# Adding the routed rows into two arrays by the parity of the tile, joined on VectorE at the end

## The chip, the cores and the metric

One core of a Trainium2 chip. The metric is the device time of one execution in microseconds (us), a median over runs. Engines are called PE (TensorE), DVE (VectorE), ACT (ScalarE), POOL (GpSimd) and SP (SyncE, which here only issues DMAs).

## What is computed

A decoder layer on 32 sequences of 128 rows of 256 float32: causal attention with 16 heads, a cross attention with rotations and a decay mask, and a mixture of experts, each followed by a residual addition and a layer norm. The change touches only how the last part's outputs are summed:

```python
x = _layernorm(x + attn(x, qkv_weights))
x = _layernorm(x + xattn(x, ctx, ctx, Wq, Wk, Wv))
# ffn(x): 8 experts, the best 2 of each row, plus one shared expert
probs = softmax(x @ gate_w + gate_b)
topk_probs, topk_idx = top_k(probs, 2)
hr    = einsum('bsd,edf->ebsf', x, rw1) + rb1          # 256 -> 512
out_e = einsum('ebsf,efd->ebsd', swiglu(hr), rw2) + rb2
routed_out = einsum('ebsd,bse->bsd', out_e, cw)        # cw: top-2 probabilities
x = _layernorm(x + shared_out + routed_out)
```

## The kernel before

The program is written engine by engine, with semaphores by hand. Each engine runs its instructions in the order written; a waiting instruction holds all behind it on its engine. There are three stages.

**Attention, both kinds (to about 450 us).** `step(n)` runs over the 32 sequences, about 11 us each, software-pipelined: GpSimd's step holds the rsqrt of two layer norms (L620, L624), `turn_into` (L590, the rotated keys) and L605, which adds the shared expert's bias to a row block. Each row's packet (256 values, its own row number, its experts and weights) is scattered by L611 to `sent`, sorted by expert.

**Routed tiles (about 470 to 793 us).** `sent` is worked off in TILES = 71 tiles of 128 packets, each of one expert. Tile i goes through all engines:

- ACT: `load` (L1184) fetches `xg` three tiles ahead, `out_x` (L1194) copies the transposed rows, `silu` (L1189), `out_h` (L1199), `weighted` (L1205) writes `yw`, the result times the row's gate.
- PE: `turn_x` (L987), `turn_h` (L994), `result` (L1010), `hidden` (L1001).
- DVE: `biased` (L1536), `weight_parts` (L1541), `out_y` (L1552), `rows_of` (L1547), which turns the packet's row number into `result_row`.
- POOL: `product` (L638), `tile_weight` (L642), `add_rows` (L654): an indirect DMA that adds the 128 rows of `yw` to `total` in memory, at the rows that `result_row` names.

A hardware loop (Fori) runs four tiles per round, with the tiles of the start and the end written out. In the turn of tile i the engines stand at different tiles: ACT applies silu to tile i, weights tile i-2 and loads i+3; DVE biases tile i and finishes tile i-2; POOL multiplies tile i and then issues the adding transfer of tile i-3. A row sits in two tiles (its two experts), and two adding transfers to the same row must not overlap. So `wait_rows(i)` holds transfer i until transfer i-1 has landed (`row_added`, 16 a transfer). `yw` has two buffers, so `weighted(i)` waits for transfer i-2; `result_row` has four, so `rows_of(i)` waits for transfer i-4.

```python
def wait_rows(i):                      # L648
    eng.wait_ge(yw_set, i + 1)
    eng.wait_ge(packet_row, i + 1)
    after(eng, row_added, 16 * i)
for n in range(4):                     # in the loop over k
    product(4 * k + n, n % 2)
    wait_rows(4 * k + n - 3)
    tile_weight(4 * k + n, n)
    add_rows((n + 1) % 4)
```

**The end (from 793 us).** SP waits for the last `row_added`, loads `total` in 8 quarters of four sequences (`fin`, L565, 512 KB each), and DVE and ACT normalise them (`moments`, `shifts`, POOL's `root` L685, `finish` L1238). For quarters 4 to 7 PE still computes the shared expert (`shared_hidden` L784, `shared_output` L804), with `shared_silu` on ACT (L1093), `shared_gate` (L1389) and `add_shared` (L1400) on DVE. SP stores each quarter (L570).

## Time and profile before

| | |
|---|---|
| median of 3 runs | 839.64 us (836.67 to 840.29) |
| profiled execution | 842.12 us |
| its span in the trace | 839.9 us |
| mean granted TensorE clock | 0.971 |
| PE busy | 725.7 us (86%) |
| DVE, ACT, POOL busy | 470.1, 450.1, 372.9 us (56, 54, 44%) |
| chain that ended last, DMA | 18%, of which the adding transfers 14% |

A line of the timeline gives start, duration, engine, source line, operation, output <- inputs, count, and in brackets the idle time of the engine before it with what ended it. DMA instructions on a queue (SPq, ACTq) are the issue, not the transfer. The granted clock is a fraction of 2.4 GHz: 1.00 is 2.4, 0.50 is 1.2.

### The profile page before, as it was taken

The numbers are of one execution on the slowest core, as the hardware profiler recorded it, in microseconds if no ns is written. First come the engines' busy times: TensorE is split into PE (matmuls) and PEld (weight loads), VectorE is DVE, ScalarE is ACT, GpSimd is POOL, SyncE is SP. The second block draws the span as 40 slices with busy tenths as digits, with TensorE's granted clock in tenths as the row PEclk, the third lists the DMA queues.
The fourth block names the chain that finished last, engine by engine and source line by source line (L and its number), as shares of the span: only waits on it lengthen the run. The fifth ranks groups of instructions, "written<-read, shape, count | busy, mean of one in ns | idle before, by whom it ended". The sixth has DMA issues, their size and how long they took to land.

```text
span 839.9 us, 19432 instructions
## 1 busy us (share of the span) xinstructions
PE 725.7 (86%) x5464; PEld 527.5 (63%) x5465; DVE 470.1 (56%) x1427; ACT 450.1 (54%) x1242; POOL 372.9 (44%) x523
## 2 busy tenths in 40 slices
PE   7969999999999999999799887877887777777893
PEld 6757888888888888888555454444444443443452
DVE  3554778988888888887555333332233333332164
ACT  0367888888888888886231143333333333332135
POOL 1001333355454455554447055555555555555211
PEclk9988999999999999999899899999999999999996
DMA  8635542123222333335435633333433334333363
GB/s 298 243 113 152 199 137 64 58 90 90 73 81 84 94 100 95 103 103 175 138 110 189 198 56 64 59 65 59 63 63 63 63 63 63 60 62 43 78 223 125
DMA packets 79479, 89.43 MB, mean 106 GB/s; under 512 B 12016, under 2 KB 72048, under 8 KB 78384
## 3 DMA queue, kind: packets, MB, share of 16 engines
q1 hardware_dynamic: 55504, 59.83, 22.8%
q0 software_dynamic: 13680, 19.20, 13.1%
q10 hardware_dynamic: 10224, 9.49, 4.2%
q8 instruction: 39, 0.64, 0.3%
q14 instruction: 32, 0.26, 0.1%
HBM read 51.71 MB, written 36.77 MB: 105 GB/s over the span
## 4 chain that ended last, share of the span: by engine, by line
PE 50%; DMA 18%; issue 13%; DVE 6%; POOL 6%; ACT 3%; ACTq 2%; SPq 1%; POOLq 0%; DVEq 0%
DMA total<-oT,result_row 14%; PE ps L764 5%; POOL total L654 5%; PE ps L1001 4%; PE ps L861 4%; PE ps L752 4%; PE ps L774 4%; PE ps L729 4%; PE ps L885 3%; PE ps L864 3%; PE ps L732 3%; PE ps L804 2%; PE ps L695 2%; PE ps L784 2%; PE ps L871 2%
## 5 line engine op out<-in xcount | busy, mean ns | idle before, releaser
L1001 PE MATMUL ps<-first_use,xgT 128*128 x284 | 142.9, 626 | 53.3 <-ACT xgT L1194 53.3
L1076 ACT ACTIVATE prob<-ps,nmax 128x128 f32<-128x128 f32 x512 | 146.9, 379 | 31.2 <-DVE nmax L1275 31.2
L654 POOL DMA_INDIRECT total<-oT,result_row x71 | 112.1, 1579 | 21.9 <-issue 9.7
L1001 PEld LDWEIGHTS ps<-first_use,xgT 128*128 128x128 f32 x284 | 49.0, 191 | 114.6 <-issue 114.5
L1205 ACT ACTIVATE oT<-yg,weight 128x256 f32<-128x256 f32 x71 | 36.1, 508 | 127.3 <-DMA total<-oT,result_row 126.6
L1275 DVE TENSOR_REDUCE nmax<-ps 128x4 f32<-128x512 f32 x128 | 82.2, 685 | 25.8 <-PE ps L752 24.8
L590 POOL TENSOR_TENSOR rot<-products 128x128 f32<-128x128 f32 x128 | 61.1, 498 | 65.3 <-DVE products L1285 65.2
L1536 DVE TENSOR_TENSOR tile_parts<-ps,attn_only 128x512 f32<-128x512 f32 x71 | 49.1, 692 | 72.5 <-issue 59.7
L1083 ACT COPY pT<-ps 128x512 f32<-128x512 f32 x128 | 76.9, 601 | 19.5 <-PE ps L764 13.6
L764 PE MATMUL ps<-tf,prob 128*128 128x128 f32 x512 | 78.8, 277 | 6.1 <-ACT pT L1083 6.1
L1547 DVE CAST result_row<-xg 128x1 uint32<-128x1 f32 x71 | 10.9, 153 | 125.6 <-DMA total<-oT,result_row 125.6
L611 POOL DMA_INDIRECT sent<-packets,pos x64 | 63.4, 990 | 36.9 <-PE ps L752 22.6
L1010 PE MATMUL ps<-first_use,ghT 128*128 x284 | 73.8, 382 | 3.1 <-ACT ghT L1199 3.1
L638 POOL TENSOR_TENSOR tile_parts<-tile_parts 128x256 f32<-128x256 f32 x71 | 52.1, 733 | 47.3 <-ACT tile_parts L1189 47.3
L764 PEld LDWEIGHTS ps<-tf,prob 128*128 128x128 f32 x512 | 59.4, 142 | 12.7 <-issue 5.0
L1194 ACT COPY xgT<-ps 128x256 f32<-128x256 f32 x71 | 26.4, 372 | 70.7 <-issue 50.7
L784 PE MATMUL ps<-prob,sw_sb 128*128 128x512 f32 x128 | 58.8, 607 | 1.8 <-DVE tile_parts L1389 1.8
L1010 PEld LDWEIGHTS ps<-first_use,ghT 128*128 128x128 f32 x284 | 48.3, 190 | 7.7 <-issue 3.9
L642 POOL TENSOR_TENSOR weight<-weight_part,xg 128x1 f32<-128x1 f32 x71 | 13.4, 189 | 84.9 <-DMA total<-oT,result_row 79.8
L987 PEld LDWEIGHTS ps<-tf,xg 128*128 128x128 f32 x142 | 16.7, 143 | 53.9 <-issue 43.3
L1285 DVE TENSOR_TENSOR products<-ps,tf 128x256 f32<-128x256 f32 x128 | 46.3, 404 | 6.9 <-PE ps L864 2.4
L624 POOL TENSOR_TENSOR rstd<-mv,neg_half 128x1 f32<-128x1 f32 x32 | 17.6, 550 | 67.3 <-DVE mv L1293 67.3
(137 smaller groups left out, 1456.6 us busy)
## 6 DMA issues: line engine op xcount, KB each, us to landing
xg<-sent ACTq DMA_DIRECT2D x68, 130.5 KB, 2.1
k_dram<-first_use SPq DMA_DIRECT2D x4, 1024.0 KB, 5.7
attn_only<-in_x_turned SPq DMA_DIRECT2D x32, 128.0 KB, 3.1
attn_only<-k_dram SPq DMA_DIRECT2D x256, 16.0 KB
attn_only<-in_x SPq DMA_DIRECT2D x32, 128.0 KB, 2.7
attn_only<-in_ctx SPq DMA_DIRECT2D x32, 128.0 KB, 2.7
first_use<-in_L_ffn_rw SPq DMA_DIRECT2D x8, 512.0 KB, 5.0
x2T_dram<-x2T SPq DMA_DIRECT2D x32, 128.0 KB, 2.6
```

Source lines behind the costliest of these rows:

```text
L590: eng.tensor_tensor(rot[:, t % 2, m + e, :], ra[:, t % 2, m + e, :], rb[:, t % 2, m + 1 - e, :], ALU.add).then_inc(done, 1)
L611: eng.indirect_dma_start(sent, bass.IndirectOffsetOnAxis(ap=pos[:, t, j:j + 1], axis=0), packets[:, t % SLOTS, :], None).then_inc(sent_in[ ...
L638: eng.tensor_tensor(gate_h[:, r, :], hid[:, r, FFN:2 * FFN], sil[:, r, :], ALU.mult).then_inc(gh_set, 1)
L654: eng.indirect_dma_start(total, bass.IndirectOffsetOnAxis(ap=result_row[:, slot:slot + 1], axis=0), yw[:, slot % 2, :], None, compute_op=A ...
L764: mm = eng.transpose(PROBT[:, n * P:(n + 1) * P], prob[:, t % 2, 4 * u + n, :], ident)
L784: mm = eng.matmul(ps[:, bank + half, :].rearrange("p (b t) -> p b t", b=QB), sw1_sb[:, c, cols:cols + P], x2T4[:, q % EARLY, :, c, :], sta ...
L1001: mm = eng.matmul(ps[:, r, :], xgT[:, r, c, :], rw1_sb[:, bass.ds(e * (DC * 2 * FFN) + c * 2 * FFN, 2 * FFN)], start=(c == 0), stop=(c == ...
L1010: mm = eng.matmul(ps[:, 4 + r, 0:D], ghT[:, r, c, :], rw2_sb[:, bass.ds(e * (FFN // P * D) + c * D, D)], start=(c == 0), stop=(c == FFN // ...
L1076: ins = eng.activation(prob[:, t % 2, 4 * u + n, :], SCORE[u][:, n * P:(n + 1) * P], ACT.Exp, bias=nmax[:, t % 2, 4 * u + n:4 * u + n + 1])
L1083: eng.copy(pT[:, u, :, :].rearrange("p n t -> p (n t)"), PROBT).then_inc(pT_set, 1)
L1275: eng.tensor_reduce(nmax[:, t % 2, 4 * u:4 * u + 4], SCORE[u].rearrange("p (h j) -> p h j", j=P), AX_X, ALU.max, negate=True).then_inc(max ...
L1536: eng.tensor_tensor(hid[:, r, :], ps[:, r, :], rb_h[:, bass.ds(e * (2 * FFN), 2 * FFN)], ALU.add).then_inc(hid_set, 1)
```

## The change

`total` becomes two arrays, `totals[0]` and `totals[1]`. The transfer of an even tile adds to the first, that of an odd tile to the second, and each waits for the transfer two tiles ahead, which is the last one into the same array. The semaphore `row_added` becomes two. `totals[0]` holds what `total` held; `totals[1]` starts as zeros, written by one more transfer on POOL at step 8. At the end SP loads both, and DVE adds the second to the first (`join`) before the moments or the shared addition of that quarter. The second half of a quarter goes to parts of `first_use` and `attn_only` that the experts' weights and biases held.

```diff
-            def wait_rows(i):
+            def wait_rows(i, r, added):
                 eng.wait_ge(yw_set, i + 1)
                 eng.wait_ge(packet_row, i + 1)
-                after(eng, row_added, 16 * i)
+                after(eng, row_added[r], 16 * added)
...
-                eng.indirect_dma_start(total, bass.IndirectOffsetOnAxis(ap=result_row[:, slot:slot + 1], axis=0),
-                                       yw[:, slot % 2, :], None, compute_op=ALU.add).then_inc(row_added, 16)
+                eng.indirect_dma_start(totals[slot % 2], bass.IndirectOffsetOnAxis(ap=result_row[:, slot:slot + 1], axis=0),
+                                       yw[:, slot % 2, :], None, compute_op=ALU.add).then_inc(row_added[slot % 2], 16)
...
-                    wait_rows(4 * k + n - 3)
+                    wait_rows(4 * k + n - 3, (n + 1) % 2, 2 * k + (n - 3) // 2)
...
+                if n == 8:
+                    eng.dma_start(totals[1][:, :].rearrange("(n p) d -> p n d", p=P),
+                                  zeros[:, 0:D].unsqueeze(1).broadcast_to([P, B + 1, D])).then_inc(idle_sent, 16)
...
-            def weighted(i, r, slot):
+            def weighted(i, r, slot, added):
-                after(eng, row_added, 16 * (i - 1))
+                after(eng, row_added[r], 16 * added)
...
-                        weighted(i - 2, n % 2, (n - 2) % 4)
+                        weighted(i - 2, n % 2, (n - 2) % 4, 2 * k + (n - 2) // 2)
...
-            def rows_of(i, slot):
-                after(eng, row_added, 16 * (i - 3))
+            def rows_of(i, slot, added):
+                after(eng, row_added[slot % 2], 16 * added)
...
-            eng.wait_ge(row_added, 16 * TILES)
+            for r in range(2):
+                eng.wait_ge(row_added[r], 16 * ((TILES + 1 - r) // 2))
             for q in range(NQ):
-                eng.dma_start(fin[:, q * QB:(q + 1) * QB, :],
-                              total[q * QB * S:(q + 1) * QB * S, :].rearrange("(b p) d -> p b d", p=P)).then_inc(fin_in[q], 16)
+                for half, place in enumerate((fin[:, q * QB:(q + 1) * QB, :], odd_of(q))):
+                    eng.dma_start(place, totals[half][q * QB * S:(q + 1) * QB * S, :].rearrange("(b p) d -> p b d", p=P)
+                                  ).then_inc(fin_in[q], 16)
...
+            def join(q):
+                eng.wait_ge(fin_in[q], 32)
+                rows = fin[:, q * QB:(q + 1) * QB, :]
+                eng.tensor_tensor(rows, rows, odd_of(q), ALU.add).then_inc(joined, 1)
...
             shared_gate(5, 0, 6)
+            join(0)
             moments(0)
+            join(1)
             shared_gate(5, 1, 0)
             moments(1)
             shifts(0)
+            join(2)
+            join(3)
+            join(4)
+            shared_gate(6, 0, 6)
             add_shared(4, 2)
-            shared_gate(6, 0, 6)
             moments(2)
             shifts(1)
+            join(5)
             shared_gate(6, 1, 0)
             add_shared(5, 4)
             moments(3)
             shifts(2)
             shared_gate(7, 0, 6)
+            join(6)
             moments(4)
             shifts(3)
             add_shared(6, 2)
+            join(7)
             shared_gate(7, 1, 0)
```

The program on POOL in the loop, two tiles of it, before (lines of before; a weight's row carries the waits of `wait_rows`):

```order
L638 TENSOR_TENSOR tile_parts<-tile_parts 128x256 [waits gh_turned,sil_set]
L411 REGISTER_ALU [waits packet_row,yw_set]
L642 TENSOR_TENSOR weight<-weight_part,xg 128x1 [waits part_set,row_added]
L654 DMA total<-oT,result_row 4224x256
L636 REGISTER_ALU
L638 TENSOR_TENSOR tile_parts<-tile_parts 128x256 [waits gh_turned,sil_set]
```

and in the changed kernel (its own line numbers):

```order
L650 TENSOR_TENSOR tile_parts<-tile_parts 128x256 [waits gh_turned,sil_set]
L418 ISA [waits packet_row,yw_set]
L654 TENSOR_TENSOR weight<-weight_part,xg 128x1 [waits part_set,row_added_even]
L666 DMA total0<-oT,result_row 4224x256
L648 REGISTER_ALU
L650 TENSOR_TENSOR tile_parts<-tile_parts 128x256 [waits gh_turned,sil_set]
L654 TENSOR_TENSOR weight<-weight_part,xg 128x1 [waits row_added_odd,part_set,packet_row,yw_set]
L666 DMA total1<-oT,result_row 4224x256
```

No instruction moved there; the semaphore waited for alternates, and with it the array.

The program on DVE at the end, from the shift of quarter 0 to the moments of quarter 2, before:

```order
L1596 SCALAR_TENSOR_TENSOR shift3<-mv3,rstd3 128x4 [waits rstd3_set]
L1400 TENSOR_TENSOR first_use<-ps,first_use 128x512 [waits sy_made,fin_in4]
L1400 TENSOR_TENSOR first_use<-ps,first_use 128x512 [waits sy_made]
L1389 SCALAR_TENSOR_TENSOR tile_parts<-ps,sb1_sb,pT 128x512 [waits sy_made,ssil_set]
L1587 BN_STATS bn3<-first_use 128x6 [waits fin_in2]
```

and in the changed kernel:

```order
L1613 SCALAR_TENSOR_TENSOR shift3<-mv3,rstd3 128x4 [waits rstd3_set]
L1596 TENSOR_TENSOR first_use<-first_use 128x1024 [waits fin_in2]
L1596 TENSOR_TENSOR first_use<-first_use 128x1024 [waits fin_in3]
L1596 TENSOR_TENSOR first_use<-first_use,attn_only 128x1024 [waits fin_in4]
L1401 SCALAR_TENSOR_TENSOR tile_parts<-ps,sb1_sb,pT 128x512 [waits sy_made,ssil_set]
L1412 TENSOR_TENSOR first_use<-ps,first_use 128x512 [waits sy_made,joined]
L1412 TENSOR_TENSOR first_use<-ps,first_use 128x512 [waits sy_made]
L1604 BN_STATS bn3<-first_use 128x6 [waits joined]
```

Three joins (L1596) now stand ahead of the shared gate of (6,0) (L1401), and that gate stands ahead of the shared addition of quarter 4 (L1412).

## Rows read from the trace of the kernel before

**Rows 1.** Busy time by stretch: us, then each engine's busy us and instructions, clock, DMA, GB/s

```profile
50.00:450.00 400.00, 381.58 (x4190) 329.57 (x4191) 312.34 (x989) 304.18 (x880) 175.40 (x282) 0.97 0.35 109
...
600.00:700.00 100.00, 78.29 (x279) 41.49 (x280) 32.29 (x95) 36.86 (x95) 58.78 (x71) 1.00 0.39 62
```

**Rows 2.** Groups by line: engine, out<-in | busy us, mean ns | idle before, releaser

```profile
L1205 ACT ACTIVATE oT<-yg,weight 128x256 f32<-128x256 f32 x71 | 36.1, 508 | 127.3 <-DMA total<-oT,result_row 126.6
...
L1547 DVE CAST result_row<-xg 128x1 uint32<-128x1 f32 x71 | 10.9, 153 | 125.6 <-DMA total<-oT,result_row 125.6
```

**Rows 3.** The adding transfer's own line: durations in ns, first and last start, landing

```profile
L654 POOL DMA_INDIRECT total<-oT,result_row x71: 1550/1579/1631, 489.1 to 789.7; - x71
...
DMA to landing us min/median/max: 3.5/3.8/4.0
```

**Rows 4.** Timeline, 624 to 644: start, us, engine line op [idle before <-releaser]

```profile
624.55 1.58 POOL L654 DMA_INDIRECT total<-oT,result_row  x1 [0.15 <-issue]
...
628.48 0.51 ACT L1205 ACTIVATE oT<-yg,weight 128x256 f32<-128x256 f32 x1 [1.53 <-DMA total<-oT,result_row]
...
629.48 0.69 DVE L1536 TENSOR_TENSOR tile_parts<-ps,attn_only 128x512 f32<-128x512 f32 x1 [0.84 <-issue]
...
630.71 0.72 POOL L638 TENSOR_TENSOR tile_parts<-tile_parts 128x256 f32<-128x256 f32 x1 [0.27 <-ACT tile_parts L1189]
...
641.13 0.51 ACT L1205 ACTIVATE oT<-yg,weight 128x256 f32<-128x256 f32 x1 [1.78 <-DMA total<-oT,result_row]
...
643.82 0.71 POOL L638 TENSOR_TENSOR tile_parts<-tile_parts 128x256 f32<-128x256 f32 x1 [0.72 <-ACT tile_parts L1189]
```

**Rows 5.** Timeline, 484 to 491, before the first transfer is waited for

```profile
484.62 1.88 PE L1001 MATMUL ps<-first_use,xgT 128*128 x4
...
487.64 1.88 PE L1001 MATMUL ps<-first_use,xgT 128*128 x4
...
488.04 0.73 POOL L638 TENSOR_TENSOR tile_parts<-tile_parts 128x256 f32<-128x256 f32 x1 [2.32 <-ACT tile_parts L1189]
...
489.06 1.63 POOL L654 DMA_INDIRECT total<-oT,result_row  x1
```

**Rows 6.** Timeline, the last tiles: transfer 65

```profile
766.73 1.58 POOL L654 DMA_INDIRECT total<-oT,result_row  x1 [0.45 <-issue]
```

**Rows 7.** Timeline of the end; last, VectorE's shared gate as in Rows 2

```profile
793.28 7.43 SPq L565 DMA_DIRECT2D first_use<-total  x8
...
797.12 1.41 DVE L1587 BATCH_NORM_STATS2 bn<-first_use 128x6 f32<-128x256 f32 x4 [5.49 <-DMA first_use<-total]
...
803.61 1.29 DVE L1400 TENSOR_TENSOR first_use<-ps,first_use 128x512 f32<-128x512 f32 x2 [1.81 <-DMA first_use<-total]
...
819.70 2.07 ACT L1238 ACTIVATE first_use<-first_use,shift,rstd 128x256 f32<-128x256 f32 x4 [2.81 <-DVE shift L1596]
...
823.28 6.46 PE L804 MATMUL ps<-sw_sb,tile_parts 128*128 128x256 f32 x16 [4.99 <-DVE tile_parts L1389]
...
L1389 DVE SCALAR_TENSOR_TENSOR tile_parts<-ps,sb_sb,pT 128x512 f32<-128x512 f32 x16 | 11.9, 748 | 23.8 <-ACT pT L1093 23.8
```

**Rows 8.** DMA issues: out<-in queue op xcount, median us from issue to landing

```profile
sent<-packets,pos POOLq DMA_INDIRECT x64, 3.1
...
sent<-zeros,tail_rows POOLq DMA_INDIRECT x2, 5.1
```

**Rows 9.** Additions with both inputs in SBUF: by line, min/median/max ns

```profile
L1515 DVE TENSOR_TENSOR passed<-counts,tf x1: 752/752/752, 459.0 to 459.0; 128x568 f32<-128x568 f32 x1
...
L1448 DVE TENSOR_TENSOR res<-att,attn_only x32: 418/701/705, 59.4 to 409.5; 128x256 f32<-128x256 f32 x32
```

**Rows 10.** Transfers of zeros by line, and GpSimd's timeline at step 8

```profile
L596 POOL DMA_DIRECT2D sent<-zeros x1 | 1.2, 1191 | 27.1 <-DVE zeros L1270 27.1
...
L598 POOL DMA_DIRECT2D total<-zeros x1 | 0.6, 622 | 0.0
...
129.27 0.88 POOL L590 TENSOR_TENSOR rot<-products 128x128 f32<-128x128 f32 x2 [3.42 <-DVE products L1285]
```

More of the change, by code:

```diff
@@ L104, in decoder_kernel @@
         k_dram = nc.dram_tensor("k_dram", (B, DH, GB, 2 * DH * NU), F32).ap()
-        total = nc.dram_tensor("total", (ROWS + P, D), F32).ap()
+        totals = [nc.dram_tensor(f"total{r}", (ROWS + P, D), F32).ap() for r in range(2)]
         x2T_dram = nc.dram_tensor("x2T_dram", (B, P, DC, P), F32).ap()
@@ L271, in decoder_kernel, with odd_of @@
         fin = first_use[:, 0:B * D].rearrange("p (b d) -> p b d", d=D)
+        def odd_of(q):
+            lo = q % 4 * QB * D
+            return (first_use[:, B * D + lo:B * D + lo + QB * D] if q < 4 else attn_only[:, lo:lo + QB * D]
+                    ).rearrange("p (b d) -> p b d", d=D)
         bn3 = sb("bn3", [P, NQ, QB, 6])
@@ L369, in decoder_kernel @@
         xg_in = [sem(f"xg_in{i}") for i in range(4)]
-        row_added = sem("row_added")
+        row_added = [sem("row_added_even"), sem("row_added_odd")]
+        joined = sem("joined")
         xg_turned = sem("xg_turned")
@@ L551, in _ @@
             eng.wait_ge(zeros_laid, 16 * (NE - TAILS_SP))
-            eng.wait_ge(idle_sent, 32)
+            eng.wait_ge(idle_sent, 48)
             for i in range(3):
@@ L597, in step @@
                                   zeros[:, :].unsqueeze(1).broadcast_to([P, IDLE, PACKET])).then_inc(idle_sent, 16)
-                    eng.dma_start(total[ROWS:ROWS + P, :], zeros[:, 0:D]).then_inc(idle_sent, 16)
+                    eng.dma_start(totals[0][ROWS:ROWS + P, :], zeros[:, 0:D]).then_inc(idle_sent, 16)
+                if n == 8:
+                    eng.dma_start(totals[1][:, :].rearrange("(n p) d -> p n d", p=P),
+                                  zeros[:, 0:D].unsqueeze(1).broadcast_to([P, B + 1, D])).then_inc(idle_sent, 16)
                 t = n - 5
@@ L661, in _ @@
                 eng.wait_ge(x2_stored[r], 16 * (B - EARLY * QB) // 2)
-            eng.wait_ge(idle_sent, 32)
+            eng.wait_ge(idle_sent, 48)
             eng.wait_ge(kept_stored, 16 * EARLY)
             product(3, 1)
-            wait_rows(0)
+            wait_rows(0, 0, 0)
             tile_weight(3, 3)
@@ L675, in _ @@
                 product(i, i % 2)
-                wait_rows(i - 3)
+                wait_rows(i - 3, (i - 3) % 2, (i - 3) // 2)
                 tile_weight(i, i % 4)
@@ L679, in _ @@
             for i in range(TILES - 3, TILES):
-                wait_rows(i)
+                wait_rows(i, i % 2, i // 2)
                 add_rows(i % 4)
@@ L1231, in _ @@
             for i in range(TILES - 2, TILES):
-                weighted(i, i % 2, i % 4)
+                weighted(i, i % 2, i % 4, i // 2)
             def finish(q):
@@ L1395, in add_shared @@
                 else:
-                    eng.wait_ge(fin_in[q], 16)
+                    eng.wait_ge(joined, q + 1)
                 for i in range(2):
```

8 lines of the change are left out of this document (4 added, 4 removed).

## The prediction

> **What bounds the kernel now.** I read the busy table by stretch first [rows 1]. In the stage of the routed tiles (from about 475 us to 793) TensorE is busy 78 us of 100 at a granted clock of 1.00, GpSimd 59, the other two a third each. Before 450 TensorE is busy 95% (381.58 of 400) and the change touches only one instruction there. The groups by line [rows 2] name who waits in the tile stage: ScalarE's weighting L1205 waits 126.6 us, VectorE's row numbers L1547 125.6 us, both for the adding transfer. The row of L654 itself [rows 3] says why: 71 transfers, the first issued at 489.1, the last at 789.7, each landing 3.8 us after its issue. That is 300.67 / 70 = 4.295 us from one to the next, and it is one latency plus a short hand-over: a transfer issued at 624.55 lets L1205 start at 628.48 (3.93 us) [rows 4], and the other 0.36 are GpSimd's weight L642 and its hand-over. So the single chain transfer, landing, transfer paces the stage, and the 3.8 us are latency, of which only 1.58 occupy GpSimd [rows 3].
>
> **What the change does to that chain.** GpSimd's wait before transfer i was for the landing of i-1; now it is for i-2, the last one into the same array. The other two waits (yw on ScalarE, result_row on VectorE) asked for i-2 and i-4 already and still do, now on the semaphore of the parity. So landing, transfer is cut, and the question is what is late next. I follow what a landing still releases, in the order of the engines' programs:
> 1. Transfer i-4 lands, ScalarE weights tile i-2 (L1205), 0.51 us.
> 2. ScalarE then issues the load of tile i+3, copies xgT and applies silu to tile i+1. VectorE's bias L1536 (629.48, ends 630.17), which sits behind the waiting L1547 on VectorE, is ready at the same moment, so both engines give the same answer.
> 3. GpSimd multiplies the gates of tile i+1 (630.71, 0.72 us) and only behind this, in program order, issues the transfer of tile i-2. From the start of L1205 at 628.48 to the end of that product at 631.43 are 2.95 us [rows 4]. Product to transfer, with the weight between and no wait, is 488.04 to 489.06, thus 0.30 beyond the product's own 0.72 [rows 5].
> 4. Transfer i-2 takes 3.93 us until L1205 of tile i can start.
>
> The cycle is 2.95 + 0.30 + 3.93 = 7.18 us, and it spans two tiles: 3.59 us each. At the seam of the hardware loop the way from L1205 (641.13) to the product's end (643.82 + 0.71) is 3.40 us, 0.45 more; it falls on one parity, once in four tiles, and the in-order engines make the other parity follow: 0.11 more per tile. **The new pace is 3.70 us**, against 4.295. Two adding transfers are then in flight for part of the time, but GpSimd writes the descriptors of the second (1.58 us) while the first moves its data.
>
> Bounds of that pace. Below: TensorE alone ran tiles every 3.02 us when no transfer was yet to be waited for (L1001 at 484.62 and 487.64) [rows 5]. GpSimd alone needs 0.72 + 0.30 + 1.58 and about 0.1, 2.7 us. Both lie below 3.70. Above: an adding transfer with a second one in flight is not in the trace. The nearest rows are two plain scatters issued back to back, 3.1 us median for the 64 of L611, and 5.1 for the two of L631 [rows 8]. I take 3.93 as it stands, because the steady spacing leaves the data phases of two transfers (3.8 - 1.58 = 2.2 us each) nearly apart; every 0.1 us of latency would cost 0.05 us a tile, 3.3 us in all.
>
> **Sum for the tile stage.** Transfers 0 to 65 (489.06 to 766.73, 277.7 us) become 65 x 3.70 = 240.5: **-37**. Transfers 66 to 70 stand outside the loop: from 766.73 to the landing (SyncE's loads at 793.28) they take 26.5 us, as each waits for the one before, about 4.6 us [rows 6, 7]. With two chains I lay them out from the transfer of tile 65: tile 66 at +2.8, tile 67 at +7.1 (behind the product of tile 70, as above), tile 68 at +8.5 (it has no product ahead of it), 69 at +11.6 (67's landing is late), 70 at +13.2, landing at +17; with the 0.3 us that these unrolled waits cost in each of the five rows, +18: **-8.5**. TensorE is in time for that: even with the shared-expert matmuls that stand between its last tiles I put the result of tile 70 at about +10, before +12 where its weighting can start.
>
> **What it adds at the end.** SyncE now loads both arrays, 16 transfers of 512 KB instead of 8, in pairs. Counted from SyncE's first issue at 793.28: the first was used at 797.12 (3.8 us), the fifth at 803.61 (10.3 us), 1.62 us each [rows 7]. Pair q is then there at 2.2 + 3.24 (q + 1): 5.4, 8.7, 11.9, 15.2, 18.4, 21.6 and so on, as against 10.3 for quarter 4 alone. Each join is an addition of 128x1024 from two SBUF inputs; the nearest row is L1515, 128x568, 752 ns [rows 9], so about 1.23 us, eight of them.
> VectorE's program, same clock: the join of quarter 4 waits until 18.4 and sits ahead of the gate of (6,0), which nothing in its data requires. Join 19.6, gate 20.4, shared addition of quarter 4 done 21.7; the moments of quarter 2 start there. From there in program order, with moments and shift 2.25 (four statistics are 1.41 of it), gate 0.75, shared addition 1.3 [rows 7]: moments 24.0, join of 5 25.2 (26.2, see below), gate (6,1) 27.0, addition 28.3, moments 30.5, gate (7,0) 31.3, join of 6 32.8, moments 35.1. ScalarE's finish of quarter 3 (2.07) and silu (7,1) (some 0.7) follow those and let gate (7,1) end at 38.6, while the addition of 6 and the join of 7 fit beside them. The last 16 matmuls L804 take 6.46 us, after 4.99 us without matmuls; that gap would be about 4 again, I take the same 6.5, and they end at 45.2, where before they ended at 36.5 (829.74), and what follows is unchanged. **Tail: +8.5.** If the loads' wait alone is hidden it is +5; if TensorE's other late groups run that slowly too, +12.
>
> In that list the join of quarter 5 starts with GpSimd's root of quarter 2 (about 1 us). In the trace the addition L1448, with both inputs in SBUF, takes 418 ns at the least and 701 at the median, where GpSimd's L590 runs beside it [rows 9]. Hence the extra microsecond there and 0.3 at quarter 6. The Trainium skill, "SBUF — State Buffer", on the shared ports, says that a VectorE instruction with two SBUF inputs and a GpSimd instruction that reads SBUF exclude each other; the trace agrees (418 against 701 ns). For the loads another page speaks against my term: "DMA: Bandwidth & Descriptors" gives 436 GB/s behind a fixed 2 us, 1.20 us for a load of 512 KB. By that the pair of quarter 4 would be there about 4 us earlier and the tail would be an estimated +5; the row says 1.62 us and it decides.
>
> **What it adds at the start.** One transfer of zeros, 4224 rows, on GpSimd at step 8. Two of its kind are in the trace: 896 rows 1.19 us to issue, 128 rows 0.62 [rows 10], so 0.74 ns a row and 3.7 us for this one. At that place, ahead of L605, it delays only what stands before the 3.42 us that GpSimd idles ahead of L590 [rows 10], which hides all but 0.3. Its 4.3 MB travel in the background and are awaited only at 470 us. I charge 0.5 us, 0 to 5 if GpSimd has to wait for room for its descriptors, since then the roots of the next layer norm are late.
>
> **Rivals.**
> - *TensorE sets the pace*: if steps 2 and 3 shrink, the floor is 3.02 plus the seam, 3.15 us. Then 65 x 0.55 = 36 us less: 767. Against it stands that the rows show the way from L1205 to the product at 2.95 us with no slack to lose.
> - *Transfers in flight lengthen each other a little*: latency 4.2 to 4.5 instead of 3.93, as the additions read and write memory and the tile loads run beside them: pace 3.84 to 3.99, and with 1 or 2 us in the last five 813 to 824.
> - *Slower*: they lengthen each other as the two of L631 did, 5.1 us to landing. Pace (2 x (5.2 + 3.25) + 0.45) / 4 = 4.34: +4 us up to tile 65, the last five -5, tail and start +9, in all 848. It decides from a landing of about 4.9 us on: there the pace is 4.24, and 8 us gained (2 and 6) meet the 9 paid. L611's 3.1 us with two in flight speaks against it.
> - *The change doesn't take the order away*: another wait (yw_set, which waits for the landing two back, or the queue itself) still lines up each transfer behind the last one; pace 4.29, only the tail and start are paid, 849. The cycle above is this wait, with two tiles in it; it would need one in it.
>
> **How the numbers follow.** -37 - 8.5 + 8.5 + 0.5 = -36.5 on the profiled execution's 842.12 (span 839.9 and 2.2 around it), 805.6. The profiled one lies 2.5 above the median of 839.64, so against the median: **803.1 us**. Chances: this case 0.75, TensorE's pace 0.07, somewhat longer transfers 0.12, much longer 0.03, order kept 0.03. Within the first case the pace may be off by 0.12 (8 us), the tail by 4 us and the start by 4: 791 to 815. The range takes in most of the longer transfers: 788 to 820. Faster by over 0.5%, about what a measurement of this kernel can tell from no change, 0.93; within 0.5% 0.01; slower 0.06.
>
> **What the profile would show.** Transfers L666 spaced unevenly in pairs, 3.7 us in the mean, landing still 3.8 us; GpSimd's weight waiting for ScalarE's silu or yw rather than the transfer; ScalarE's wait at the weighting still there but below 100 us; SyncE's loads issued near 748 us, and 55 us from there to the end; VectorE waiting about 2 us for the pair of quarter 4. A landing above 4.5 us or a spacing near 4.3 would prove me wrong; a spacing near 3.1 would mean the cycle is shorter than I read it.

## The result and the profile after

The kernel after takes 802.25 us (median of 4 runs, 801.57 to 807.89), the kernel before beside it 839.96 us (4 runs, 836.67 to 842.14): a ratio of 0.957, 95% interval [0.952, 0.962]. That is faster, by about the amount forecast (803.1). The profiled execution took 801.57 us with a span of 799.7.

First the busy table by stretch, then the adding transfer's own line (durations in ns, first and last start, who waited for it in us and times, time to landing).

```profile
600.00:700.00 100.00, 87.55 (x329) 50.01 (x328) 37.04 (x108) 41.74 (x108) 67.10 (x84) 1.00 0.45 73
```

```profile
L666 POOL DMA_INDIRECT total<-oT,result_row x71: 1550/1580/1631, 486.4 to 739.5; - x71
...
who waited for it (us, times):
  ACT oT L1217: 78.9, 64
...
DMA to landing us min/median/max: 3.6/3.8/4.4
```

TensorE is busy 87.55 us of 100 at the same granted clock of 1.00, against 78.29 in [rows 1]. The 71 transfers now span 253.1 us instead of 300.7, that is 3.615 us from one to the next, and each still lands after 3.8 us [rows 3]. The transfer costs what it cost; it is waited for less. ScalarE's weighting waited 126.6 us for it in [rows 2] and 78.9 now. It still waits, so the landing has not left the path.

GpSimd's timeline of four tiles, and ScalarE's weightings of the same stretch (start, us, engine line, idle before and its releaser):

```profile
600.76 1.57 POOL L666 DMA_INDIRECT total<-oT,result_row  x1 [0.16 <-issue]
602.76 0.72 POOL L650 TENSOR_TENSOR tile_parts<-tile_parts 128x256 f32<-128x256 f32 x1 [0.42 <-ACT tile_parts L1201]
603.45 0.18 POOL L654 TENSOR_TENSOR weight<-weight_part,xg 128x1 f32<-128x1 f32 x1
603.79 1.58 POOL L666 DMA_INDIRECT total<-oT,result_row  x1 [0.16 <-issue]
607.22 0.71 POOL L650 TENSOR_TENSOR tile_parts<-tile_parts 128x256 f32<-128x256 f32 x1 [1.85 <-ACT tile_parts L1201]
...
608.25 1.57 POOL L666 DMA_INDIRECT total<-oT,result_row  x1 [0.16 <-issue]
```

```profile
604.62 0.51 ACT L1217 ACTIVATE oT<-yg,weight 128x256 f32<-128x256 f32 x1 [1.68 <-DMA total<-oT,result_row]
...
607.62 0.51 ACT L1217 ACTIVATE oT<-yg,weight 128x256 f32<-128x256 f32 x1 [0.31 <-DMA total<-oT,result_row]
```

This is the cycle of the forecast. The transfer of 600.76 lets the weighting start at 604.62 (3.86 us); silu and then the product (607.22) follow it, and the product ends at 607.93, 3.31 us after the weighting began; the transfer two tiles on starts at 608.25, 0.32 later. That is 7.49 us for two tiles. The other parity goes 603.79, 607.62, 611.10: 7.31. The weight L654 no longer waits before a transfer; the product waits for ScalarE's silu, which stands behind the weighting that waits for the landing.

The end, as SyncE's loads, VectorE and TensorE show it:

```profile
743.14 10.14 SPq L574 DMA_DIRECT2D first_use<-total  x9
```

```profile
762.28 1.22 DVE L1596 TENSOR_TENSOR first_use<-first_use,attn_only 128x1024 f32<-128x1024 f32 x1 [1.78 <-DMA attn_only<-total]
763.43 0.74 DVE L1401 SCALAR_TENSOR_TENSOR tile_parts<-ps,sb_sb,pT 128x512 f32<-128x512 f32 x1
...
776.73 0.75 DVE L1401 SCALAR_TENSOR_TENSOR tile_parts<-ps,sb_sb,pT 128x512 f32<-128x512 f32 x1 [2.71 <-ACT pT L1105]
...
783.32 0.75 DVE L1401 SCALAR_TENSOR_TENSOR tile_parts<-ps,sb_sb,pT 128x512 f32<-128x512 f32 x1 [0.39 <-ACT pT L1105]
```

```profile
784.21 5.36 PE L816 MATMUL ps<-sw_sb,tile_parts 128*128 128x256 f32 x16 [4.65 <-DVE tile_parts L1401]
```

Counted from 743.14, the join of quarter 4 starts at 19.1 after a wait for its second load, the last gate at 40.2, the last matmuls end at 46.4 and the span at 56.6. Before, the same way from SyncE's first load (793.28, [rows 7]) to the end of the span took 46.6.

The balance between the two profiled executions:

| stretch | before | after | difference | forecast |
|---|---|---|---|---|
| start of transfer 0 | 489.06 | 486.42 | -2.6 | +0.5 |
| transfers 0 to 65 | 277.7 | 239.7 | -38.0 | -37 |
| transfer 65 to SyncE's loads | 26.5 | 17.1 | -9.5 | -8.5 |
| loads to end of span | 46.6 | 56.6 | +10.0 | +8.5 |
| around the span | 2.2 | 1.9 | -0.3 | 0 |

One profile of this study, that of the kernel with one semaphore below, is of an execution slower than the timed ones (862.06 us against a median of 851.59), mostly before the tiles; its spacing and tail are read, its time is not.

The first row is no effect of the change that I could tell: the programs of this study are nearly alike up to there (one transfer of zeros more or less, and the order of the first products), and transfer 0 starts between 483.5 and 497 us, up to 4.3 us apart for kernels that ran on one chip, and 12 with that slower profile. So the experiments below are compared by the spacing of the transfers (first to last start, by 70) and the tail (SyncE's first load to the end of the span), and by their ratio to the kernel before on their own chip.

### The profile page after: what moved, and what is told of

Same layout as the page of the kernel before. It is cut to its first block, busy times and chain, and to the rows that moved or that the text cites. A ratio compares the mean times of both kernels' runs of the same rounds, so it can differ in the third digit from the quotient of the medians.

```text
span 799.7 us, 19370 instructions
## 1 busy us (share of the span) xinstructions
PE 710.9 (89%) x5464; PEld 527.2 (66%) x5465; DVE 480.7 (60%) x1435; ACT 449.2 (56%) x1242; POOL 374.1 (47%) x524
## 4 chain that ended last, share of the span: by engine, by line
PE 45%; issue 14%; DMA 13%; POOL 9%; DVE 8%; SPq 4%; ACT 3%; DVEq 1%; ACTq 1%; POOLq 1%
DMA total<-oT,result_row 9%; POOL total L666 7%; PE ps L776 5%; PE ps L764 4%; PE ps L873 4%; PE ps L786 4%; PE ps L741 4%; PE ps L876 3%; PE ps L744 3%; PE ps L897 3%; PE ps L816 2%; PE ps L796 2%; PE ps L883 2%; PE ps L935 2%; DVE products L1297 2%
## 5 line engine op out<-in xcount | busy, mean ns | idle before, releaser
L1013 PE MATMUL ps<-first_use,xgT 128*128 x284 | 137.3, 606 | 26.9 <-ACT xgT L1206 26.7
L666 POOL DMA_INDIRECT total<-oT,result_row x71 | 112.1, 1579 | 14.3 <-issue 12.5
L1013 PEld LDWEIGHTS ps<-first_use,xgT 128*128 128x128 f32 x284 | 50.7, 189 | 77.3 <-issue 75.7
L650 POOL TENSOR_TENSOR tile_parts<-tile_parts 128x256 f32<-128x256 f32 x71 | 51.1, 720 | 93.9 <-ACT tile_parts L1201 93.9
L1217 ACT ACTIVATE oT<-yg,weight 128x256 f32<-128x256 f32 x71 | 36.1, 508 | 81.7 <-DMA total<-oT,result_row 78.9
L999 PEld LDWEIGHTS ps<-tf,xg 128*128 128x128 f32 x142 | 17.1, 140 | 51.9 <-DMA xg<-sent 25.4
L1564 DVE TENSOR_TENSOR yg<-ps,attn_only 128x256 f32<-128x256 f32 x71 | 30.0, 423 | 29.0 <-PE ps L1022 22.3
```

What stands on the lines that cost most here:

```text
L650: eng.tensor_tensor(gate_h[:, r, :], hid[:, r, FFN:2 * FFN], sil[:, r, :], ALU.mult).then_inc(gh_set, 1)
L666: eng.indirect_dma_start(totals[slot % 2], bass.IndirectOffsetOnAxis(ap=result_row[:, slot:slot + 1], axis=0), yw[:, slot % 2, :], None, c ...
L1013: mm = eng.matmul(ps[:, r, :], xgT[:, r, c, :], rw1_sb[:, bass.ds(e * (DC * 2 * FFN) + c * 2 * FFN, 2 * FFN)], start=(c == 0), stop=(c == ...
```

## Experiments

Three groups ran, each beside the kernel before on its chip (medians 848.0, 845.8 and 840.5 us). Spacing and tail are from the profiles.

| kernel | us | ratio to before | spacing | tail |
|---|---|---|---|---|
| before | 839.96 | 1 | 4.295 | 46.6 |
| after | 802.25 | 0.957 | 3.615 | 56.6 |
| after again | 810.41 | 0.959 | 3.604 | 56.4 |
| order back by added waits | 873.65 | 1.030 | 4.53 | 54.8 |
| order back by one semaphore | 851.59 | 1.012 | 4.35 | 56.2 |
| transfer ahead of the product | 798.58 | 0.942 | 3.42 | 56.0 |
| the same with one array | 876.36 | 1.031 | 4.73 | 45.5 |
| transfer two tiles behind | 776.76 | 0.916 | 3.157 | 56.3 |
| the same with one array | 853.93 | 1.014 | 4.52 | 48.0 |
| no second loads, no joins | 805.21 | 0.953 | 3.62 | 51.3 |
| no second loads, joins kept | 805.22 | 0.951 | 3.64 | 52.5 |
| joins in another order | 806.56 | 0.950 | 3.62 | 51.1 |
| before with after's gate order | 842.69 | 1.003 | 4.33 | 47.0 |
| two tiles behind and joins reordered | 765.39 | 0.914 | 3.156 | 51.2 |

### Is it the wait, or the second array?

The theory is that the gain comes from the wait for the landing one back alone. The first test puts that wait back beside the new one.

```
                 after(eng, row_added[r], 16 * added)
+                after(eng, row_added[1 - r], 16 * (added + r))
```

> Two arrays, loads and joins as in the changed kernel, but each adding transfer again waits for the one just before it too (tile i-1). My theory, that the gain is the wait and nothing else: the spacing of the transfers goes back to 4.29 us and only the price of the end (10 us by the trace of the changed kernel) is left, 848 to 851 us. The rival, that two arrays make the transfers themselves cheaper: well under 840, towards 802.

Measured: 873.65 us, ratio 1.030 [1.022, 1.038]; the gain is gone, but where a ratio of 1.01 was foreseen, 2% more is lost. The landing is unchanged (3.8 us). GpSimd's timeline shows a part of the rest:

```profile
605.58 0.19 POOL L654 TENSOR_TENSOR weight<-weight_part,xg 128x1 f32<-128x1 f32 x1 [1.32 <-DMA total<-oT,result_row]
606.01 1.58 POOL L667 DMA_INDIRECT total<-oT,result_row  x1 [0.23 <-issue]
...
610.20 0.19 POOL L654 TENSOR_TENSOR weight<-weight_part,xg 128x1 f32<-128x1 f32 x1 [1.73 <-DVE result_row L1560]
610.84 1.58 POOL L667 DMA_INDIRECT total<-oT,result_row  x1 [0.45 <-issue]
```

Between weight and transfer GpSimd idles 0.45 us in two turns of four, where it was 0.15 [rows 4]; that time lies on the chain from landing to landing. Over the 71 tiles it is 23.0 us, 12.5 in the kernel after. The trace doesn't say which instruction takes it: the same 0.45 us stand ahead of transfer 65 of the kernel before [rows 6], where no wait was added. But this edit changes two things, the order and the number of waits, so I made it again with one semaphore for both arrays and no wait more than before (the waits on ScalarE and VectorE count on it too).

```
-        row_added = [sem("row_added_even"), sem("row_added_odd")]
+        row_added = sem("row_added")
...
-                after(eng, row_added[r], 16 * added)
+                after(eng, row_added, 16 * i)
```

> Two arrays, two loads, joins and second zeros as in the kernel after, but one semaphore for both arrays, so transfer i waits for the landing of i-1 with no wait more than the kernel before had. Theory (the wait makes the gain, and what the first reversal cost above 850 came from its added waits): spacing of the adding transfers 4.29 us as before, landing 3.8, tail of 55 to 56 us from SyncE's loads to the end, ratio 1.008 to 1.015. Rival (two arrays in themselves slow a transfer, as the first reversal could also be read): spacing about 4.5, ratio about 1.03. Rival (two arrays in themselves bring part of the gain): spacing below 4.2, ratio below 1.00.

Measured: 851.59 us, ratio 1.012 [1.009, 1.015]. Its transfers:

```profile
L665 POOL DMA_INDIRECT total<-oT,result_row x71: 1550/1580/1632, 495.7 to 800.3; - x71
...
DMA to landing us min/median/max: 3.7/3.9/4.4
```

The theory stands: with two arrays, both loads and the joins, but the old wait, the spacing is 4.35 (4.30 and 4.33 in two profiles with one array; the granted clock is 1.00 from 500 to 700 us) and the time is that of the kernel before plus the tail. The further loss of the first test went with its added wait, whatever its mechanism. Two arrays by themselves leave the landing at 3.9 us, where it was 3.8.

### What paces the stage afterwards?

The forecast says the product in front of the transfer, behind silu and the weighting, closes the cycle. So GpSimd issues the transfer ahead of the product.

```
                 for n in range(4):
-                    product(4 * k + n, n % 2)
                     wait_rows(4 * k + n - 3, (n + 1) % 2, 2 * k + (n - 3) // 2)
                     tile_weight(4 * k + n, n)
                     add_rows((n + 1) % 4)
+                    product(4 * k + n, n % 2)
```

> The changed kernel, with GpSimd's weight and adding transfer of a tile put ahead of the product of gates instead of behind it. My theory, that the pace of 3.69 us is a cycle of two tiles through landing, weighting, VectorE's bias, silu, product, transfer: silu and product (1.05 us) leave the cycle, it becomes 2.2 + 3.93 + the seam, 3.2 to 3.3 us a tile, near TensorE's own 3.15: spacing 3.2 to 3.3, time 772 to 780. The rival, that two transfers in flight are limited by the queue or the memory: spacing stays at 3.6 to 3.7 and the time at 800 to 803.

Measured: 798.58 us, ratio 0.942 [0.933, 0.950], spacing 3.42; 13 us below what 0.957 would be on this chip (812), half of what I expected. The waits for the landing fell as foreseen (the weighting's from 78.9 to 25.7 us), but GpSimd's timeline shows what took their place.

```profile
603.03 1.58 POOL L666 DMA_INDIRECT total<-oT,result_row  x1 [0.15 <-issue]
604.07 1.30 POOL L650 TENSOR_TENSOR tile_parts<-tile_parts 128x256 f32<-128x256 f32 x1
606.37 0.19 POOL L654 TENSOR_TENSOR weight<-weight_part,xg 128x1 f32<-128x1 f32 x1 [0.99 <-DVE weight_part L1553]
606.71 1.58 POOL L666 DMA_INDIRECT total<-oT,result_row  x1 [0.15 <-issue]
```

The product, which TensorE needs for its next matmuls, now ends 2.34 us behind the start of the transfer, and the weight in front of the transfer waits for VectorE's part of the same tile, which comes behind TensorE's hidden layer. So the 1.58 us that GpSimd spends on a transfer lie in TensorE's own cycle. The same exchange in the kernel before, with one array:

> The kernel before (one array, each transfer waits for the one before), with the same exchange of product and transfer on GpSimd. My theory: its chain runs transfer, landing, weight, transfer and has no product in it, so nothing changes, 838 to 842. The rival, that the product's place costs time by itself whatever the chain: 810 to 820.

Measured: 876.36 us, ratio 1.031 [1.024, 1.039], where I expected a small change at most; spacing 4.73. The wait for the landing stands in front of the product there, so TensorE waits for it:

```profile
PE ps L994 <- POOL tile_parts L638: 29.6, 21, 2.0
```

(the waits from 600 to 700 us: waiting line, releaser, us in total, times, longest). That comes back to the transfer by way of VectorE, whose row number stands behind TensorE's result in its program. The group of the transfers from 500 to 790 us:

```profile
L654 POOL DMA_INDIRECT total<-oT,result_row x61 | 96.3, 1578 | 30.8 <-DVE result_row L1547 19.9 <-issue 9.9 <-ACT oT L1205 1.0
```

Before the exchange GpSimd idled 11.1 us ahead of as many transfers. The 19.7 us more are 0.32 us a tile, of the 0.44 by which the spacing grew. The exchange helps only where the landing has been taken off GpSimd's way first.

The other way to open the cycle leaves the product in front and brings the transfer nearer: the transfer of tile i-2 behind the product of tile i, instead of i-3. Weighting and transfer of one tile are then neighbours in the cycle, and the landing has a tile more before yw is written again.

```
                     product(4 * k + n, n % 2)
-                    wait_rows(4 * k + n - 3, (n + 1) % 2, 2 * k + (n - 3) // 2)
+                    wait_rows(4 * k + n - 2, n % 2, 2 * k + (n - 2) // 2)
                     tile_weight(4 * k + n, n)
-                    add_rows((n + 1) % 4)
+                    add_rows((n + 2) % 4)
```

It ran beside a repeat of the kernel after as its measure.

> The changed kernel once more, as the yardstick on this chip for the runs beside it. Ratio to the kernel before 0.957 as the first time; spacing of the transfers 3.6 to 3.7 us.

Measured: 810.41 us, ratio 0.959 [0.953, 0.966], spacing 3.604, tail 56.4: the same kernel within the uncertainty of 0.957.

> The changed kernel, but GpSimd issues the adding transfer of tile i-2 behind the product of tile i, not that of tile i-3. My theory: the transfer then follows its weighting at once (ScalarE weights tile i-2 in the same turn), the product of the next tile no longer stands between them, and unlike the exchange of the second run TensorE's product is not held up by 1.6 us of transfer. The cycle through the landing is 0.5 + 0.35 + 3.93, 2.4 us a tile, and TensorE or GpSimd sets the pace: spacing 3.15 to 3.3 us, 25 to 33 us less than the changed kernel beside it. The rival, that transfers in flight limit each other: landing above 4.3 us and a spacing of 3.5 or more.

Measured: 776.76 us, ratio 0.916 [0.910, 0.923], 33.6 us below the repeat and 8% below the kernel before. Its busy row from 600 to 700 and its transfers:

```profile
600.00:700.00 100.00, 97.36 (x379) 59.05 (x377) 40.90 (x126) 48.35 (x127) 78.28 (x96) 1.00 0.53 82
```

```profile
L666 POOL DMA_INDIRECT total<-oT,result_row x71: 1547/1582/1622, 493.3 to 714.3; - x71
...
who waited for it (us, times):
  ACT oT L1218: 0.8, 1
```

TensorE is busy 97% and a tile takes 3.157 us. That is the floor that the forecast had put at 3.15 for TensorE alone, and each transfer still lands after 3.8 us in the fastest kernel below, which has the same spacing; the weighting has waited for a landing once, 0.8 us in all, where it was 78.9. The cause of the pace of 3.6 is thereby shown: it was the distance of three tiles between product and transfer, which puts silu and the product of a later tile between a landing and the next transfer. Whether the distance is worth anything without the second array:

> The kernel before with the transfer of tile i-2 instead of i-3 behind the product of tile i; one array, each transfer still waits for the last. Theory (with one array the chain transfer, landing, transfer sets the pace and the distance in tiles plays no part): spacing 4.2 to 4.3 us, ratio 0.99 to 1.005. Rival (the distance alone is worth something, whatever the arrays): spacing below 4.0, ratio below 0.975. Rival (the shorter distance brings the landing into TensorE's path, as the transfer ahead of the product did): spacing above 4.5, ratio above 1.02.

Measured: 853.93 us, ratio 1.014 [1.009, 1.019], spacing 4.52. Neither the theory nor the first rival holds; the spacing is the last rival's, the ratio falls short of its 1.02:

```profile
POOL weight L642 <- DMA total<-oT,result_row: 60.0, 33, 2.3
...
PE ps L995 <- POOL tile_parts L638: 41.0, 34, 1.7
```

(two rows of the waits from 550 to 700 us). GpSimd waits for the landing and TensorE waits for GpSimd's product. One array with the nearer transfer is 1.4% slower than one array as it was; two arrays with it are 8% faster than the kernel before. The two edits can't be judged one without the other.

### What is the longer tail made of?

The tail grew by 10 us. Two kernels take parts of it away, a third tests the order in the kernel before, and a fourth keeps all parts and changes their order. The first leaves out the loads of the second array and, in place of each join, copies one element, so that the rows of odd tiles are missing in the output. The second leaves out those loads too but adds as before (what it adds is not loaded).

```
-                for half, place in enumerate((fin[:, q * QB:(q + 1) * QB, :], odd_of(q))):
+                for half, place in enumerate((fin[:, q * QB:(q + 1) * QB, :],)):
...
-                eng.wait_ge(fin_in[q], 32)
+                eng.wait_ge(fin_in[q], 16)
...
-                eng.tensor_tensor(rows, rows, odd_of(q), ALU.add).then_inc(joined, 1)
+                eng.tensor_copy(bn3[:, q, 0, 0:1], fin[:, q * QB, 0:1]).then_inc(joined, 1)
```

> The changed kernel without the second set of loads and with each join replaced by a copy of one element (the odd tiles' rows are left out of the result). Prices the end: from SyncE's first load to the end 46 to 47.5 us as before the change, 8 to 10 us less than the changed kernel beside it.

Measured: 805.21 us, ratio 0.953 [0.946, 0.961], tail 51.3 us, not the 46 to 47.5 that I expected; 5.2 us below the repeat, not 8 to 10.

> The changed kernel with all joins but without the second set of loads (what is joined is whatever lies in those places, so the odd tiles' rows are left out of the result). If the wait for the pairs of quarters 3 and 4 is what costs, most of the 10 us goes: end 48 to 51 us after SyncE's first load. If the eight additions on VectorE cost by themselves (9.8 us of work), it stays at 54 to 56.

Measured: 805.22 us, ratio 0.951 [0.945, 0.957], tail 52.5, between the two expectations. From 56.4 (the repeat on this chip; the first profile has 56.6, so these are good to a few tenths) 3.9 us go when the loads go and 1.2 more with the additions; each is read from one profile, and the two medians are the same. Above the 46.6 of the kernel before, 4.7 us are left without either. In the kernel without loads and joins the gates stand so:

```profile
752.35 7.91 SPq L574 DMA_DIRECT2D first_use<-total  x8
```

```profile
762.27 0.75 DVE L1401 SCALAR_TENSOR_TENSOR tile_parts<-ps,sb_sb,pT 128x512 f32<-128x512 f32 x1 [3.44 <-ACT pT L1105]
767.73 0.75 DVE L1401 SCALAR_TENSOR_TENSOR tile_parts<-ps,sb_sb,pT 128x512 f32<-128x512 f32 x1 [2.53 <-ACT pT L1105]
...
786.56 0.75 DVE L1401 SCALAR_TENSOR_TENSOR tile_parts<-ps,sb_sb,pT 128x512 f32<-128x512 f32 x1 [1.46 <-ACT pT L1105]
```

The gates of (5,1), (6,0) and (7,1) come 9.9, 15.4 and 34.2 us behind the first load. In the kernel before, they came 5.8, 11.5 and 29.1 us behind it:

```profile
799.06 0.75 DVE L1389 SCALAR_TENSOR_TENSOR tile_parts<-ps,sb_sb,pT 128x512 f32<-128x512 f32 x1
804.82 0.74 DVE L1389 SCALAR_TENSOR_TENSOR tile_parts<-ps,sb_sb,pT 128x512 f32<-128x512 f32 x1
...
822.38 0.75 DVE L1389 SCALAR_TENSOR_TENSOR tile_parts<-ps,sb_sb,pT 128x512 f32<-128x512 f32 x1 [1.51 <-ACT pT L1093]
```

Either the order is to blame (the kernel after takes gate (6,0) ahead of the shared addition of quarter 4) or the place: the shared expert's matmuls of the end stand in TensorE's program behind the routed tiles, and the loads now come 9.5 us earlier against them. The kernel before with that order alone:

```
-            add_shared(4, 2)
             shared_gate(6, 0, 6)
+            add_shared(4, 2)
```

> The kernel before with one edit: VectorE takes the gate of (6,0) ahead of the shared addition of quarter 4, as in the kernel after. No second array, no joins. In the kernel after without second loads and joins the tail was 51.3 us against 46.6 before. If that order makes those 4.7 us, the tail here is 50 to 51 us and the ratio 1.004 to 1.006; if they come from the last adding transfers landing earlier against TensorE's shared work, the tail stays at 46.6 (within 1) and the ratio at 1.000 within its interval.

Measured: 842.69 us, ratio 1.003 [1.001, 1.005], tail 47.0. The ratio lies between the two expectations, the tail within half a microsecond of the 46.6 before, and its gates (5,1) and (6,0) at 6.0 and 11.5:

```profile
790.48 8.22 SPq L565 DMA_DIRECT2D first_use<-total  x8
```

```profile
796.48 0.75 DVE L1389 SCALAR_TENSOR_TENSOR tile_parts<-ps,sb_sb,pT 128x512 f32<-128x512 f32 x1
801.94 0.75 DVE L1389 SCALAR_TENSOR_TENSOR tile_parts<-ps,sb_sb,pT 128x512 f32<-128x512 f32 x1 [2.72 <-ACT pT L1093]
```

So the order costs some 0.4 us of the 4.7, no more than these tails scatter, and the place is left for the rest. It fits the 4.2 us by which gate (5,1), which the order can't touch, has moved. TensorE's rows fit too, first those of the kernel before, then those of the kernel without loads and joins:

```profile
778.30 1.13 PE L1010 MATMUL ps<-first_use,ghT 128*128 x4 [0.56 <-ACT ghT L1199]
...
793.41 7.03 PE L784 MATMUL ps<-prob,sw_sb 128*128 128x512 f32 x16
```

```profile
744.91 1.13 PE L1022 MATMUL ps<-first_use,ghT 128*128 x4 [0.56 <-ACT ghT L1211]
...
757.91 7.03 PE L796 MATMUL ps<-prob,sw_sb 128*128 128x512 f32 x16
```

The last routed matmul ended 13.9 us ahead of SyncE's first load before and ends 6.3 us ahead of it now; the group of 16 shared matmuls started 0.1 us behind that load before and starts 5.6 us behind it now. TensorE is busy for 31.98 of the 32 us from 746 to 778, so it can't follow. No run moved the place alone, but this is the likely limit of a kernel without loads and joins.

It is not a part of the 10 us of the kernel after, though. The kernel with one semaphore has that kernel's loads, joins and order, and its landings come as late against TensorE as before the change:

```profile
788.63 1.12 PE L1021 MATMUL ps<-first_use,ghT 128*128 x4 [0.56 <-ACT ghT L1210]
```

```profile
804.02 8.46 SPq L573 DMA_DIRECT2D first_use<-total  x9
```

```profile
842.45 0.75 DVE L1400 SCALAR_TENSOR_TENSOR tile_parts<-ps,sb_sb,pT 128x512 f32<-128x512 f32 x1 [0.39 <-ACT pT L1104]
```

The load starts 14.3 us behind TensorE's last routed matmul. If the place made 4.7 us of the growth, the tail would be near 52 us here; it is 56.2, and gate (7,1) comes 38.4 us behind the first load, 9.3 us later than before the change. (Of its tail, 1.4 us are the last matmuls: 6.74 us at a granted clock of 0.50, against 5.36 in the kernel after.) The kernel with the added wait, whose load starts 15.7 us behind that matmul, has 54.8. So loads, joins and their order on VectorE make 8 to 10 us by themselves, and the place costs next to nothing beside them. There are two limits, and the later one counts: VectorE's program at about 56 us, and TensorE's shared work at about 51, which shows only when loads and joins are gone.

The last kernel keeps loads and joins whole and moves only their places on VectorE: gate (6,0) and the moments of quarter 2 ahead of the joins of 3 and 4, and every shift, gate and moment for which something waits ahead of the next join.

```
             join(2)
-            join(3)
-            join(4)
             shared_gate(6, 0, 6)
-            add_shared(4, 2)
             moments(2)
             shifts(1)
-            join(5)
+            join(3)
+            shifts(2)
+            join(4)
+            add_shared(4, 2)
             shared_gate(6, 1, 0)
+            join(5)
...
```

> The changed kernel, with another order of the same instructions on VectorE at the end: the gate of (6,0) and the moments and shift of quarters 1 and 2 no longer stand behind the joins of quarters 3 and 4, and each shift comes before the gate whose silu stands behind that shift's finish on ScalarE. My theory, that the 10 us at the end are waits by program order and not bytes: gate (7,1) is ready 33 us after the first load instead of 40, and 5 to 8 us are won, 794 to 797. The rival, that the second set of loads bounds the end: 801 to 803.

Measured: 806.56 us, ratio 0.950 [0.943, 0.957], tail 51.1. The kernel before took 848.0 us on this chip, so the ratio of 0.957 would be about 812: 5.3 us are won, as the theory had it, and gate (7,1) starts 33.1 us behind the first load. Of eight joins the first alone finds its data missing, for 2.8 us.

That the tail equals that of the kernel without loads and joins (51.3) doesn't mean that they are free here. TensorE's last matmuls end 37.6 us behind the first load, against 41.1 there, so another limit holds. The busy rows from 775 to 795 us (SyncE's loads start at 752.2 and 752.4), first with the joins in the new order, then without loads and joins:

```profile
775.00:795.00 20.00, 10.87 (x41) 7.44 (x40) 19.01 (x57) 8.31 (x16) 4.93 (x4) 0.92 0.52 178
```

```profile
775.00:795.00 20.00, 13.38 (x41) 9.11 (x40) 14.06 (x54) 9.37 (x18) 4.03 (x4) 0.83 0.32 111
```

VectorE (the third pair of numbers) is busy 19.0 us of 20, against 14.1: the additions now run without waiting, but they fill its time. What went are the waits by program order. What the new order would give without joins, no run tells.

### Both together

> Transfer of tile i-2 behind the product of tile i, and VectorE's joins in the order that won 5.3 us at the end of the kernel after. If the two gains lie in different stages, as I hold, they add: spacing 3.16 us, tail 51 us, ratio 0.916 - 0.006 = 0.910. If the faster tile stage makes the shared work wait more, the tail stays at 55 to 56 and the ratio at 0.916.

Measured: 765.39 us (762.22 to 771.58), ratio 0.914 [0.909, 0.918], spacing 3.156, tail 51.2. Spacing and tail show both gains, in their different stages, and the faster tile stage did not lengthen the tail. The ratio alone can't tell the second gain: it is 0.914 against 0.916, and 0.910 was expected. This is the fastest kernel of the study, about 4.5% below the kernel after by the two ratios.

## Why the prediction was right, step by step

- **The binding wait.** Right. With the old wait restored and nothing else changed the gain is gone (spacing 4.35), and with the new one it is 3.6.
- **The cycle of two tiles, 3.70 us a tile.** Right in mechanism and size: 3.69 over transfers 0 to 65. In the four tiles above, the weighting starts 3.83 to 3.90 us after the transfer (forecast 3.93), the product ends 2.85 to 3.31 after the weighting's start (2.95, and 3.40 at the seam), and the transfer follows 0.32 later (0.30). Transfers come in uneven pairs, as forecast: 3.03, 4.46, 2.85 and 4.21 us apart.
- **The latency with two in flight.** I took it unchanged, on the argument that one's data phase ends before the other's begins. It is 3.8 us, also at a spacing of 3.157; the rivals that lengthened it fall.
- **The last five transfers, 18 us.** 17.1.
- **The tail, +8.5.** It came to +10.0, and the sum hides a step that failed. The pair of quarter 4 was there at 19.1 against 18.4, and gate (6,0) at 20.3 against 20.4. Then gate (7,0) started at 33.6 us instead of 30.5: I let VectorE alone set it, but it waits for ScalarE's silu (2.71 us idle in the row above), and that stands behind the finish of quarter 2, which needs VectorE's shifts(2). The order among the engines goes round once more than I drew it. Part of this was given back by the last matmuls, 5.36 us where I kept 6.46. Charging the growth to loads, joins and their order was right: the two kernels with the old wait, whose landings come as late against TensorE as before, still grow by 8.2 and 9.6 us. What the forecast lacked is a second limit behind that one. I listed +5 for the case that the loads' wait is hidden, and the kernels without loads and joins, or with the joins in another order, came to +4.5 to +5.9, but for reasons that I hadn't drawn: TensorE's shared work doesn't move up with the landings, and VectorE's own work fills the end.
- **The join behind GpSimd's root.** Half right. I gave the extra microsecond to VectorE's join of quarter 5; the trace gives it to GpSimd's root, there (the second row) and already at the join of quarter 2:

```profile
757.14 1.99 POOL L697 TENSOR_TENSOR rstd<-var,neg_half 128x4 f32<-128x4 f32 x1 [3.27 <-DVE var L1609]
...
767.37 1.98 POOL L697 TENSOR_TENSOR rstd<-var,neg_half 128x4 f32<-128x4 f32 x1 [8.24 <-DVE var L1609]
```

  The other six roots take 1.0 us. These two start 0.09 us behind a join (757.05 and 767.28), whose 1.22 us are what a join takes alone. The Trainium skill, "SBUF — State Buffer", section "Who interferes with whom", states that the two engines exclude each other at their common port and that whoever issues first keeps it for the whole instruction; both rows agree.
- **The zeros, +0.5.** The issue took 1.91 us, not the 3.7 that I estimated from two rows [rows 10], and GpSimd still idles 2.05 us behind it. What it costs the whole can't be told from the scatter of the first row of the balance.

```profile
125.21 1.91 POOL L609 DMA_DIRECT2D total<-zeros  x1
...
129.85 0.88 POOL L599 TENSOR_TENSOR rot<-products 128x128 f32<-128x128 f32 x2 [2.05 <-DVE products L1297]
```

- **The rate of the final loads.** From 755 to 770 us the trace shows 348 to 350 GB/s, which is 1.50 us for 512 KB, where I took 1.62; the first pair came at 6.3 us instead of 5.4, and the two errors nearly cancel at quarter 4. I had set the rate of "DMA: Bandwidth & Descriptors" of the Trainium skill, 436 GB/s, against my term, and misapplied it: the page fits that figure to transfers issued from GpSimd, and in its section "Bandwidth" it says that between HBM and SBUF the memory side binds, at about 358 GB/s for each core. By that a load of 512 KB is an estimated 1.46 us, and the trace agrees.

That the median came within 1 us of the forecast is partly luck. Against the forecast of 805.6 us for the profiled execution it took 801.57: the start gave 3.1 us that I hadn't forecast and can't explain, the tile stage and the last transfers 1 us each, 0.3 came from around the span, and the tail took back 1.5. The interval of the ratio alone spans some 9 us.

Of the rivals, TensorE's pace (767 us) did not hold for this kernel: it is the next floor, and two kernels of this study reached it.

## What to carry to other kernels

Splitting an accumulation in two takes a latency off the path only down to the next cycle that still contains it. Draw that cycle through all in-order programs, with the tile number beside each step: here a landing still released a product two tiles ahead before the next transfer could go, and one tile less of distance was worth nearly as much as the second array. Ask the same at the end: work that nothing in its data holds back (a gate behind a join) costs as long as it stands there, and such a stage can have a second limit just behind the first. What goes when a part is taken away is therefore not that part's share of the growth; a run that puts the other suspect back (here the old wait, with loads and joins kept) tells the two apart.

## What the runs showed of the chip beside this

- Two adding transfers in flight, the starts a mean of 3.16 and at the least 2.64 us apart, landed after 3.8 us in the median, as one alone did (the fastest kernel, 3.7/3.8/4.2 least, median, most).
- Between a weight and its transfer GpSimd idled 0.15 us in the loop of the kernel before, and 0.45 in two turns of four with a wait added, but 0.45 also where none was added (transfer 65 of the kernel before, [rows 6]). What takes the 0.3 us is open.
- GpSimd's rows overlap behind a transfer: a product that follows it at once is listed from 1.03 us after the transfer's start with 1.30 us, while it takes 0.72 elsewhere. Both together take 2.34 us, against 1.58 + 0.72 = 2.30, so the pair takes no longer than its parts.
- A transfer of zeros of 4224 rows (4.3 MB) took GpSimd 1.91 us to issue, of 896 rows 1.19 [rows 10]: the time isn't proportional to the rows.
